# A graph network on one core: the edge scatter begins in the loop of ranks, and the woven stage works in halves

## What is computed

```python
edge_index = jnp.stack([src, dst])
h = jnp.maximum(_layernorm(x, axis=-1), 0.0)
x = x + _L0_gnn_ref(h, edge_weight, src, dst, L0_gnn_beta, L0_gnn_eps)
...
norm_h = feat / jnp.maximum(norm, 1e-12)
e = beta[0] * edge_weight
seg_max = jax.ops.segment_max(e, src, num_segments=n)
ex = jnp.exp(e - seg_max[src])
seg_sum = jax.ops.segment_sum(ex, src, num_segments=n)
p = ex / seg_sum[src]
msg = norm_h[src] * p[:, None]
h = jax.ops.segment_sum(msg, dst, num_segments=n)
return (1.0 + eps[0]) * feat + h
```

## Time and profile before

| | us |
|---|---|
| median of 3 runs (lowest, highest) | 6825.32 (6819.9, 6832.18) |
| profiled execution | 6829.46 |
| its span | 6828.0 |
| PE busy | 4951.0 (73%) |
| DVE busy | 4675.9 (68%) |
| POOL busy | 2614.4 (38%) |
| ACT busy | 1634.4 (24%) |
| L954, matmuls of the chunks, x2816 | 857.6 |
| L790, the scatter, x816 | 830.1 |
| L848, the gather, x816 | 1027.0 (758.0 and 269.0) |

### The profile page before, as it was taken

One profiled execution on the slowest core, in us unless ns is written; L12 is line 12 of the kernel. 1 busy time (PEld: TensorE's weight loads), 2 busy tenths in 40 slices (PEclk: granted clock), 3 DMA queues, 4 the chain that ended last, 5 costly groups with the idle time before them and its releaser, 6 DMA issues. The chain is left out here.

```text
span 6828.0 us, 71514 instructions
## 1 busy us (share of the span) xinstructions
PE 4951.0 (73%) x19096; PEld 3093.0 (45%) x19096; DVE 4675.9 (68%) x6628; ACT 1634.4 (24%) x3088; POOL 2614.4 (38%) x2433
## 2 busy tenths in 40 slices
PE   2777774258888886997888897788868886555555
PEld 1255553235555554785333277333324443333333
DVE  7699999957777776798999989899981101111112
ACT  0044442023333200323455410355530003000000
POOL 0177777778888885000000000000000000777774
PEclk9999999999999998656999965899999998555555
DMA  2000002434343311453333356233326666222221
GB/s 78 7 8 8 8 8 58 113 107 135 124 133 128 109 43 35 141 159 101 113 114 111 106 155 186 89 113 113 112 76 241 241 241 165 53 53 53 53 53 45
DMA packets 427374, 681.15 MB, mean 100 GB/s; under 512 B 86757, under 2 KB 308611, under 8 KB 417355
## 3 DMA queue, kind: packets, MB, share of 16 engines
q1 hardware_dynamic: 349282, 569.41, 25.9%
q0 software_dynamic: 77808, 107.93, 6.4%
HBM read 536.29 MB, written 140.87 MB: 99 GB/s over the span
## 5 line engine op out<-in xcount | busy, mean ns | idle before, releaser
L1043 POOL DMA_INDIRECT ring<-rel_dram,rel_col x782 | 744.4, 952 | 3345.7 <-SPq L71 3107.6
L954 PE MATMUL total<-to,from 128*128 128x256 f32 x2816 | 857.6, 420 | 228.5 <-issue 140.8
L790 POOL DMA_INDIRECT cells_dram<-rec,place x816 | 830.1, 1017 | 451.9 <-issue 242.7
L1077 PE MATMUL total<-ring,onehot 128*128 x1612 | 541.5, 498 | 455.7 <-DMA ring<-rel_dram,rel_col 452.0
L1612 PE MATMUL sums<-acc,hw 128*64 128x400 f32 x2144 | 759.5, 510 | 140.2 <-DVE acc L1546 139.7
L848 POOL DMA_INDIRECT ring<-l_dram,src_pair x600 | 758.0, 1263 | 182.9 <-issue 182.9
L1054 DVE TENSOR_SCALAR onehot<-iota,loc_pair 128x128 f32<-128x128 f32 x806 | 177.2, 286 | 816.9 <-PE total L1077 816.9
L954 PEld LDWEIGHTS total<-to,from 128*128 128x128 f32 x2816 | 467.1, 195 | 573.0 <-issue 545.8
L1077 PEld LDWEIGHTS total<-ring,onehot 128*128 128x128 f32 x1612 | 402.8, 310 | 594.8 <-issue 532.7
L1612 PEld LDWEIGHTS sums<-acc,hw 128*64 128x64 f32 x2144 | 269.1, 138 | 596.0 <-issue 316.5
L545 PE MATMUL node<-moved,onehot 128*128 128x75 f32 x1584 | 365.8, 426 | 221.6 <-DVE moved L419 221.6
(11 more groups left out here) (389 smaller groups left out, 8038.8 us busy)
## 6 DMA issues: line engine op xcount, KB each, us to landing
count<-ac_dram SPq DMA_DIRECT2D x200, 800.0 KB, 4.3
strip<-ac_dram SPq DMA_DIRECT2D x75, 1600.0 KB, 7.1
ac_dram<-stage SPq DMA_DIRECT2D x125, 640.0 KB, 3.5
h<-ac_dram SPq DMA_DIRECT2D x26, 1600.0 KB, 8.0
acc<-ac_dram SPq DMA_DIRECT2D x24, 1600.0 KB, 8.4
lo_row<-lo_dram SPq DMA_DIRECT2D x102, 256.0 KB, 3.5
rel_dram<-rows SPq DMA_DIRECT2D x25, 1024.0 KB, 5.4
mask_dram<-mask SPq DMA_DIRECT2D x25, 800.0 KB, 5.0
```

What stands on the lines that cost most here:

```text
L790: pool.indirect_dma_start(m.cells_dram[:, :], bass.IndirectOffsetOnAxis(ap=m.place[:, j:j + 1], axis=0), m.rec[:, j, :], None, bounds_chec ...
L954: nc.tensor.matmul(spots[:, at(spot), :].rearrange("p o n -> p (o n)"), from_[:, n % 2, u, :], to[:, n % 2, u, :, :].rearrange("p k d -> p ...
L1043: pool.indirect_dma_start(ring[:, c % SLOTS, :], None, m.rel_dram[:, :], bass.IndirectOffsetOnAxis(ap=m.rel_col[:, c:c + 1], axis=0)).then ...
L1077: last = nc.tensor.matmul(total[:, at(col, D)], onehot[:, j % U, :], rows, start=False, stop=False, skip_group_check=True)
```

## The change

1. In `cells` the place of a block of pairs is worked out (`settle`) as soon as its 7 groups are ranked, on 128x128 instead of 128x896, and POOL scatters the first HEAD = 80 pairs while later blocks are ranked; POOL must have these landed before it leaves the phase. `sort_edges` does the other 736.
2. The codes behind the tables are computed ahead of the loop on 128x11 instead of 1x1408, go through memory (`cell_dram`, now two rows), and are packed into words inside the loop. A word holds four places and the segment number above them; `need_row` is gone.
3. The normalisation of x moves from `source_softmax` into the loop, between groups 3 and 32; its sums of squares go to ACT.
4. In the woven stage `mark` works on four chunks (128x512), PE waits for halves, gets the segment number by a shift from the word that it has anyway, and loads `near_row` once for two groups.

```diff
+            pool.wait_ge(blanked, 64)
+            pool.wait_ge(placed, 1)
+            for j in range(HEAD):
+                pool.indirect_dma_start(m.cells_dram[:, :], bass.IndirectOffsetOnAxis(ap=m.place[:, j:j + 1], axis=0), m.rec[:, j, :], None,
+                                        bounds_check=P * NCH - 1, oob_is_err=False).then_inc(scattered, 16)
+            pool.wait_ge(scattered, 16 * HEAD)
...
+                if g % per_block == per_block - 1:
+                    dve.wait_ge(select, g + 1)
+                    settle(g // per_block)
+                if g == 3:
+                    step(v.tensor_reduce(total[:, :], m.x[:, :, :], AX.X, ALU.add))
+                    step(v.tensor_scalar(total[:, :], total[:, :], 1.0 / D, None, ALU.mult))
+                if g == 9:
+                    v.tensor_tensor(m.h[:, :, :], m.x[:, :, :], bc(total[:, :], D), ALU.subtract).then_inc(centred, 1)
+                if g == 18:
+                    dve.wait_ge(measured, NT)
+                    v.tensor_scalar(var[:, :], var[:, :], 1.0 / D, EPS, ALU.mult, ALU.add).then_inc(var_ready, 1)
+                if g == 20:
+                    dve.wait_ge(root, 1)
+                    step(v.reciprocal(var[:, :], var[:, :]))
+                    step(v.tensor_tensor(m.h[:, :, :], m.h[:, :, :], bc(var[:, :], D), ALU.mult))
+                if g == 23:
+                    v.tensor_scalar(m.h[:, :, :], m.h[:, :, :], 0.0, None, ALU.max).then_inc(bent, 1)
+                if g == 32:
+                    dve.wait_ge(measured, 2 * NT)
+                    v.tensor_scalar(m.norm[:, :], m.norm[:, :], 1e-24, None, ALU.max).then_inc(n2, 1)
+                if g == 36:
+                    dve.wait_ge(cells_in, 32)
+                    step(v.memset(word[:, :], 0.0))
+                if 36 <= g < 36 + G:
+                    c = g - 36
+                    step(v.scalar_tensor_tensor(word[:, :], code_row[:, c::G], float(SPOTS) ** c, word[:, :], ALU.mult, ALU.add))
+                if g == 43:
+                    step(v.scalar_tensor_tensor(word[:, :], need[:, :], float(SPOTS) ** G, word[:, :], ALU.mult, ALU.add))
+                    step(v.tensor_copy(m.spot_row[:, :], word[:, :]))
...
+    done = HEAD // G
+    for gi in range(done, ITERS * R):
...
-            def mark(n):
-
-                b, cols = n % 2, slice(n * BB, (n + 1) * BB)
...
+            def mark(k):
+
+                b, cols = k // 2 % 2, slice(k * G, (k + 1) * G)
+                half = slice(k % 2 * G, (k % 2 + 1) * G)
...
-                dve.wait_ge(summed, n * BB + BB)
-                if n + 2 < TURNS:
-                    mark(n + 2)
+                for k in (2 * n, 2 * n + 1):
+                    dve.wait_ge(summed, k * G + G)
+                    if n + 2 < TURNS:
+                        mark(k + 4)
...
+                return pe.snap(word >> (4 * G), min_val=1, max_val=LAST)
...
-                            if c == 1:
-                                next_need = need_of(k + 1)
+                            if c == G - 1:
+                                next_need = need_of(next_word)
```

More of the change, by code:

```diff
@@ L247, in _ @@
                 step(v.scalar_tensor_tensor(near[:, :], own[:, :], D * 4.0 ** k, near[:, :], ALU.mult, ALU.add))
-            step(v.tensor_copy(m.near_row[:, :], near[:, :]))
+            step(v.scalar_tensor_tensor(near[:, 0::2], near[:, 1::2], 64.0, near[:, 0::2], ALU.mult, ALU.add))
+            step(v.tensor_copy(m.near_row[:, :], near[:, 0::2]))
             step(v.tensor_scalar(own[:, :], tile_first[:, 0::G], float(D), None, ALU.mult))
@@ L449, in _ @@
             step = Chain(dve, e_)
[L450 to L462, removed]
             step(v.tensor_scalar(den[:, :], m.seg_sum[:, :], 0.5, None, ALU.max))
-            dve.wait_ge(root2, 1)
-            step(v.tensor_tensor(den[:, :], den[:, :], norm[:, :], ALU.mult))
+            step(v.tensor_tensor(den[:, :], den[:, :], m.norm[:, :], ALU.mult))
             step(v.reciprocal(den[:, :], den[:, :]))
@@ L567, in _ @@
                 last.then_inc(told, 1)
+HEAD = 80
 def cells(nc, m):
@@ L720, in _ @@
-            halves = [slice(k * (NCH // 2), (k + 1) * (NCH // 2)) for k in range(2)]
-            number = hi_i[0:1, 0:NCH // 2]
-            for half in halves:
-                step(v.tensor_copy(number, cell_all[0:1, half]))
-                step(v.tensor_scalar(number, number, 41, None, ALU.mult))
-                step(v.tensor_scalar(number, number, 10, None, ALU.arith_shift_right))
-                step(v.tensor_copy(row_tile[:, half], number))
-            step(v.scalar_tensor_tensor(place, row_tile, -float(NT), cell_all[0:1, :], ALU.mult, ALU.add))
@@ L735, in _ @@
-            for half in halves:
-                step(v.tensor_copy(number, seg[:, half]))
-                step(v.tensor_scalar(number, number, BUFS - 1, None, ALU.bitwise_and))
-                step(v.tensor_copy(quarter[:, half], number))
-            step(v.scalar_tensor_tensor(spot, quarter, float(ROOM), place, ALU.mult, ALU.add))
-            step(v.memset(word, 0.0))
-            for k in range(G):
-                step(v.scalar_tensor_tensor(word, spot[:, k::G], float(SPOTS) ** k, word, ALU.mult, ALU.add))
@@ L743, in _ @@
-            step(v.tensor_copy(m.spot_row[:, :], word))
-            step(v.tensor_scalar(seg, seg, 1.0, None, ALU.add))
-            step(v.tensor_copy(m.need_row[:, :], seg[:, G - 1::G]))
+                if g % per_block == per_block - 1:
[4 more added lines that the diff above has]
+                    step(v.tensor_scalar(total[:, :], total[:, :], 1.0 / D, None, ALU.mult))
@@ L918, in _ @@
             dve.wait_ge(rec_in, 16)
-            mark(0)
-            mark(1)
+            for k in range(4):
+                mark(k)
             for n in range(TURNS):
```

155 lines of the change are left out of this document (93 added, 62 removed).

## The result

The changed kernel takes **6649.99 us** (median of 4 runs, 6641.57 to 6658.1); the kernel before took 6827.57 beside it (4 runs, 6819.9 to 6832.18). The ratio is **0.9742, 95% interval 0.9727 to 0.9756**: some 177 us faster, where 203 were forecast. The two profiled executions are 6652.4 and 6828.0 us long, 175.6 apart.

What follows compares the result with a forecast made beforehand. POOL's scatter was taken to end the softmax, PE narrowly ahead of POOL the woven stage. Gains of 4.5 + 75 + 124 = 203 us off 6828.0 gave 6625, range 6585 to 6665, chance 0.63.

Steps and rivals of the forecast that it cites:

- Cells: Ranking phase: early scatters were to let POOL leave at 309.5 us instead of 314.0, despite added DVE work; gain 4.5 us.
- Softmax: Softmax phase: with scatters and normalisation moved out, the bound goes from POOL's scatter to DVE; gain 75 us.
- Woven stage: Fewer register loads on PE and shorter marks delaying POOL's gathers less were to gain 124 us, bounds 60 and 140.
- So PE again ends the stage, narrowly: Woven stage: PE's sum of 1168 us was to stay the bound, with POOL at 1143 to 1231.
- a transfer of POOL's that begins while DVE runs an instruction with two operands in SBUF waits for the end of that one instruction: Rule for POOL's gathers and scatters: after that wait each takes its usual time; marks of about 0.60 us instead of 1.14.
- 352 halves by 0.3 us are 106 us: Woven stage: POOL's total gather delay from half-length marks, added to 1021 us, giving 1127 against 1275.
- PE's pace: Woven stage: PE's sum of 1292 us, less 36 and less 88, was to be 1168.
- the term for the loads: Woven stage: fewer register loads save PE net 0.5 us a turn, 80 us over 160 turns and some 8 more.
- 36 had been counted for waits: Woven stage: the last 48 turns or so would be 36 us shorter by PE's own pace, if POOL gets faster.
- The mechanism of the first: Rival, woven stage: POOL stays the bound as halves run together or DVE is late; 1232 us, total 6690; chance 0.17.
- The second: Rival: POOL's delays don't shrink, having another cause; woven stage stays 1292 us, total 6746; chance 0.09.
- The third: Rival, woven stage: register loads aren't what holds PE, so only 36 us of waiting go; total 6710; chance 0.08.

## Why the prediction was right, and where not

**Cells.** 2.9 us instead of 4.5. The loop ended at 289.7 (forecast about 288), the scatter ran from 193.1 to 302.4 (191 to 300), three transfers were held for long, by 7.1 us together (7). The steps held; that leaving the phase costs POOL 9 us held too (8.7), and it makes POOL's last scatter, not DVE, the end of the phase.

**Softmax.** 71 instead of 75, for the right reason: the bound went from POOL to DVE, which idles 1.52 us at the barrier instead of 48.56. 1017.1 us where 1013.3 were summed. That it was the moved scatters which freed the phase is argued from these rows; the run with `HEAD` 0 meant to show it fell on a slow chip. An estimate from the rows: POOL's last scatter ends at 1273.9, and 80 more at 1.307 us each would have ended near 1378, behind DVE's 1326.7.

**Woven stage.** 102 instead of 124, and here two steps failed, of which the first set the time.
- "So PE again ends the stage, narrowly" was wrong. POOL ends it. The step is the rule that "a transfer of POOL's that begins while DVE runs an instruction with two operands in SBUF waits for the end of that one instruction". It can miss the changes from one to the next in an unbroken run, and then waits for the end of a half's third mark, mostly the end of the run. The term is "352 halves by 0.3 us are 106 us": measured were 152, of which 92.8 come from missed changes; the rest, 59.5, is less than forecast, since 62 gathers that began in the first 0.04 us of a mark weren't held: the range held partly by luck, two errors of opposite sign. I had given halves that run together 0.55 us of delay twice a turn, not 3.1 at a time. POOL's time was 1174 instead of 1127. Shown by the marks made narrow (mean gather 0.947, none above 1.07) and by the runs with waits or one-hots between them (no long gather in five).
- PE's pace was mis-sized: 1168 forecast to PE's last matmul, 1122.8 in the run without the gathers, 169 less than before instead of 124. The steps from chunk to chunk within a turn (means of turns 2 to 175) show the term for the loads: the seven of a turn took 5.14 us before and 4.54 in that run, 0.60 less where 0.5 was forecast. That was near by luck: the loads of `spot_row` and `need_row` gave 0.23 and not 0.48, since the step with the check moved into it grew by 0.26 to 0.40; the two steps at which `near_row` is loaded gave 0.36 and not 0.15. So 106 us instead of 88. The other 63, where 36 had been counted for waits, lie between the turns and weren't taken apart further; the granted clock was 0.97 before and 0.99 in that run.

**The rivals.** The mechanism of the first (POOL stays the bound with part of the gain, since halves run together) is what happened, with 22 us of it instead of 65; the time falls into the forecast's own range. The second is out: the Trainium skill ("SBUF — State Buffer", Who interferes with whom) infers that `tensor_tensor` leaves descriptor generation alone, and a gather of 1.134 us falls to 0.947 when nothing but the width of `tensor_tensor` is cut. The third is out: the loads hold PE, since an added load with its check lengthened PE's step by 0.44 to 0.46 us (0.52 was taken). DVE as the bound was far, at 0.69 us a mark and 0.605 from one to the next.

## What to carry to other kernels

Where an engine's long instructions hold another's transfers, look at the longest unbroken run of them, not at one: splitting each into halves helps (125 us here) until the engine falls behind and runs them together. A short instruction of another kind between any two is enough to let the transfer in. When two engines stand within a few per cent of each other, taking work from one alone can even lose (packed words alone: 22 us), so undo each part singly before crediting it. Before work is moved into an earlier phase, compare when each engine is done there: 64 scatters instead of 80, done at 282 us, would let DVE end it at 293 (an estimate; the run with 64 fell on a slow chip).

## What the runs showed of the hardware

- A gather on GpSimd's queue takes 0.947 us undisturbed and up to 4.6 when it starts just ahead of or in a run of six `tensor_tensor` of 0.605 us pitch with both operands in SBUF; with 0.12 us more between their starts, or a short `tensor_scalar` between two, the delay ends with the instruction in which it began.
- A `tensor_tensor` of 128x512 with one operand in PSUM (L907, L948) held no gather: 197 began in one before the change and 107 after, all at their undisturbed time.
- A phase whose last work is a scatter ends 8.7 us after it, one whose last work is DVE's after 0.56.
- A register load with its bounds check lengthened PE's step from one chunk to the next from 0.53 us to between 0.97 and 0.99 (medians).
- Three chips, in later runs, took the kernel before 18 to 19% longer (8067 to 8133 us) than two earlier series of runs (6826 and 6828). In the variants traced there DVE got about a tenth of its usual instructions done while GpSimd scattered, and its usual number afterwards; the cause is open.
